# A DLRM tower on one core: ten chunk turns spread over the pass, and the second gram packed in quadrants between compares

## The reference

```python
e = jnp.stack([tbl_0[ids[:, 0]], ..., tbl_31[ids[:, 31]]], axis=1)   # (2048, 32, 128)
dot_products = jnp.einsum('bfd,bgd->bfg', e, e)
z = dot_products[:, iu, ju]                       # the 496 pairs above the diagonal
h = jnp.concatenate([z, dense_ctx], axis=1)       # 496 + 16 = 512
h = jnp.maximum(h @ W_top1 + b_top1, 0.0)
h = jnp.maximum(h @ W_top2 + b_top2, 0.0)
y = h @ W_top3
```

## Time and profile before

| | |
|---|---|
| median of 3 runs | 629.28 us (628.71 to 630.79) |
| the profiled execution | 625.68 us |
| its span, first to last instruction | 623.8 us |
| mean granted TensorE clock | 0.88 |
| PE, DVE, ACT, POOL busy | 447.8, 256.7, 126.5, 327.2 us |
| one pass of the loop (the fourth of six, 345.3 to 417.6 us) | 72.3 us |

### The profile page before, as it was taken

One profiled execution on the slowest core, in us unless ns is written; L12 is line 12 of the kernel. 1 busy time (PEld: TensorE's weight loads), 2 busy tenths in 40 slices (PEclk: granted clock), 3 DMA queues, 4 the chain that ended last, 5 costly groups with the idle time before them and its releaser, 6 DMA issues.

```text
span 623.8 us, 11340 instructions
## 1 busy us (share of the span) xinstructions
PE 447.8 (72%) x4692; PEld 406.2 (65%) x4692; DVE 256.7 (41%) x486; ACT 126.5 (20%) x220; POOL 327.2 (52%) x324
## 2 busy tenths in 40 slices
PE   0766311685779677886669867896877867798988
PEld 0766200675768577775669866685867757698967
DVE  2686000374407453373515544073533635158420
ACT  2452000012212122112211221121221122113313
POOL 6787777256643776346662566436763366620000
PEclk9998655797889987897998878898888978999999
DMA  7996312033321233012240223113421123311000
GB/s 164 245 232 172 100 50 55 14 56 73 76 56 35 67 71 80 26 46 59 73 82 17 59 68 76 50 38 63 76 77 28 42 63 74 77 26 27 1 4 1
DMA packets 31294, 42.10 MB, mean 67 GB/s; under 512 B 11077, under 2 KB 24141, under 8 KB 31273
## 3 DMA queue, kind: packets, MB, share of 16 engines
q1 hardware_dynamic: 18936, 20.64, 15.5%
q0 software_dynamic: 10240, 20.99, 13.3%
q10 hardware_dynamic: 2096, 0.17, 0.3%
HBM read 41.77 MB, written 0.01 MB: 67 GB/s over the span
## 4 chain that ended last, share of the span: by engine, by line
PE 50%; issue 15%; DVE 13%; another core or an unknown queue 12%; POOL 7%; DMA 2%; DVEq 0%; ACT 0%; POOLq 0%
PE sel_ps L289 19%; PE gram_ps L308 13%; PE work_ps L342 8%; POOL gathered L240 7%; DVE onehot L614 7%; DVE pairs L631 6%; PE work_ps L350 4%; PE work_ps L271 2%; DMA gathered<-table,tile_ids 2%; PE work_ps L420 1%; PE work_ps L333 1%; PE gram_ps L317 1%; PE work_ps L429 1%; PE work_ps L325 1%
## 5 line engine op out<-in xcount | busy, mean ns | idle before, releaser
L240 POOL DMA_INDIRECT gathered<-table,tile_ids x320 | 327.0, 1022 | 227.7 <-PE work_ps L271 110.1
L289 PE MATMUL sel_ps<-onehot,table_hi 125*128 125x256 f32 x768 | 213.6, 311 | 82.8 <-DVE onehot L614 36.8
L289 PEld LDWEIGHTS sel_ps<-onehot,table_hi 125*128 125x128 f32 x768 | 163.0, 212 | 90.5 <-issue 49.1
L614 DVE TENSOR_SCALAR onehot<-id_rows,row_no 128x512 fp32r<-128x512 int32 x384 | 160.2, 484 | 141.8 <-remote 80.3
L289 PE MATMUL sel_ps<-onehot,table_lo 125*128 125x256 f32 x768 | 206.9, 303 | 3.6 <-issue 3.6
L289 PEld LDWEIGHTS sel_ps<-onehot,table_lo 125*128 125x128 f32 x768 | 163.1, 212 | 6.6 <-issue 6.4
L631 DVE STREAM_TRANSPOSE pairs<-gram_ps 32x1024 f32<-32x1024 f32 x56 | 69.8, 1246 | 174.8 <-PE gram_ps L308 174.2
L308 PE MATMUL gram_ps<-rows_T 128*64 128x64 f32 x1792 | 80.5, 249 | 62.1 <-issue 62.1
L308 PEld LDWEIGHTS gram_ps<-rows_T 128*64 128x64 f32 x1792 | 72.3, 162 | 73.4 <-issue 73.0
L479 ACT ACTIVATE rows_T<-sel_ps 128x512 f32<-128x512 f32 x48 | 30.1, 627 | 221.5 <-remote 90.4
L470 ACT ACTIVATE rows_T<-work_ps 128x512 f32<-128x512 f32 x80 | 45.7, 594 | 136.7 <-PE work_ps L271 118.6
(11 more groups left out here) (26 smaller groups left out, 95.3 us busy)
## 6 DMA issues: line engine op xcount, KB each, us to landing
id_rows<-ids_selected SPq DMA_DIRECT2D x48, 256.0 KB
gathered<-table,tile_ids POOLq DMA_INDIRECT x320
pairs<-tables_selected SPq DMA_DIRECT2D x6, 448.0 KB
x<-tables_selected SPq DMA_DIRECT2D x6, 448.0 KB
w_sb<-w SPq DMA_DIRECT2D x1, 1024.0 KB
w_sb<-w SPq DMA_DIRECT2D x1, 512.0 KB
pairs<-tables_selected SPq DMA_DIRECT2D x6, 52.0 KB
x<-tables_selected SPq DMA_DIRECT2D x6, 52.0 KB
```

Of the source, the lines that this page charges most:

```text
L240: nc.gpsimd.indirect_dma_start(gathered[:, t, g, :], None, tables_gathered[g], bass.IndirectOffsetOnAxis(ap=slot_id, axis=0)).then_inc(chu ...
L289: last_op = nc.tensor.matmul(sel_ps[:, u % 2, e, :], part[0:SEL_P, 2 * u + e, k, :], onehot[0:SEL_P, h, kk, e, :], start=(e == 0 and k == ...
L614: last_op = nc.vector.tensor_scalar(onehot[:, h, kk, :, :].rearrange("p e s -> p (e s)"), id_rows[:, slot, :, :].rearrange("p e s -> p (e ...
```

## The change

The ten turns are put singly between the other work of PE. The new order of a pass is: turn 0; select 1; turn 1; pairs 0; select 2; turn 2; select 3; turn 3; select 4; turn 4; pairs 1; select 5; turn 5; first half of layer 1; turn 6; gram 0; turn 7; second half of layer 1; turn 8; select 0 of the next pass; turn 9; layer 2; gram 1; layer 3. The banks of `work_ps` are given out anew, and each turn from the third on waits for the move of the chunk before it. ScalarE's order follows.

On VectorE the pack falls into three functions. Gram 0 is still turned and merged at once, between compares 0 and 1 of the next pass. Gram 1 is turned in the next pass: two quadrants ahead of compare 2, one ahead of compare 3, one ahead of compare 4, and merged ahead of compare 5. The wait for `x0_done` is gone. In the last pass gram 0 is formed as in the loop (64 columns for each matmul) and no longer as singles. The diff:

```diff
--- before.py
+++ after.py
@@ -120,8 +120,8 @@
         gram_ps = psum("gram_ps", [P, 4 * 16 * N_FEAT])
         work_ps = psum("work_ps", [P, 2, CHUNK, P])
 
-        chunk_bank = [0, 1, 0, 0, 1, 0, 0, 1, 0, 1]
-        pairs_bank = [1, 1]
+        chunk_bank = [0, 1, 1, 0, 1, 1, 1, 1, 1, 1]
+        pairs_bank = [0, 0]
 
         def layer_ps(bank, n):
             return work_ps[:, bank, 2 * n:2 * n + 2, :].rearrange("p a s -> p (a s)")
@@ -248,25 +248,16 @@
                 first, n = CHUNKS[c]
                 pe.wait_ge(chunk_in[t][c], at(i, o, 16 * n, 16 * n))
 
-                if cc == 0 and not known_first(i, o):
-
-                    pass
-                elif cc == 1 and not known_first(i, o):
+                if cc == 1 and not known_first(i, o):
 
                     pe.wait_ge(sel_moved, at(i, o, UNITS, 1))
-                elif cc in (3, 6, 8):
-                    pe.wait_ge(chunk_moved, at(i, o, 2 * NC, {3: 3, 6: 6, 8: 7}[cc]))
-                elif cc == 2:
-                    pe.wait_ge(chunk_moved, at(i, o, 2 * NC, 1))
-                elif cc == 5:
-                    pe.wait_ge(chunk_moved, at(i, o, 2 * NC, 4))
-                elif known_first(i, o) and cc > 1:
-
-                    pe.wait_ge(chunk_moved, {4: 2, 7: 5, 9: 8}[cc])
-                elif cc in (4, 7):
-                    pe.wait_ge(x0_ready, at(i, o - 1, 2, {4: 1, 7: 2}[cc]))
-                elif cc == 9:
-                    pe.wait_ge(x1_ready, at(i, o - 1, 2, 1))
+                elif cc == 3 and known_first(i, o):
+                    pe.wait_ge(chunk_moved, 1)
+                elif cc == 3:
+                    pe.wait_ge(x0_ready, at(i, o - 1, 2, 1))
+                elif cc >= 2:
+
+                    pe.wait_ge(chunk_moved, at(i, o, 2 * NC, 3 if cc == 4 else cc))
                 for g in range(n):
                     last_op = nc.tensor.transpose(work_ps[:, chunk_bank[cc], g, :], gathered[:, t, first + g, :],
                                                   ident[:, :])
@@ -292,10 +283,10 @@
                                                            stop=(e == 1 and k == SEL_K - 1 and part is table_lo))
                     last_op.then_inc(onehot_used, 1)
 
-            def gram_waits(i, o, t, both=False):
+            def gram_waits(i, o, t):
                 pe.wait_ge(chunk_moved, at(i, o, 2 * NC, NC * (t + 1)))
                 pe.wait_ge(sel_moved, at(i, o, UNITS, UNITS))
-                if not (known_first(i, o) and t == 0) and not (both and t == 1):
+                if not (known_first(i, o) and t == 0):
 
                     pe.wait_ge(gram_read, at(i, o, 2, t))
 
@@ -339,7 +330,7 @@
                 for n in range(2):
                     for k in range(K1):
                         first = (2 * m + n) * P
-                        last_op = nc.tensor.matmul(layer_ps(1 - m, n), w1_sb[:, k, first:first + P],
+                        last_op = nc.tensor.matmul(layer_ps(0, n), w1_sb[:, k, first:first + P],
                                                    x0[:, k, :], start=(k == 0), stop=(k == K1 - 1))
                 last_op.then_inc(x1_done, 1)
 
@@ -351,36 +342,31 @@
                                                    x1[:, k, :], start=(k == 0), stop=(k == K2 - 1))
                 last_op.then_inc(x2_done, 1)
 
-            def selects(i, o):
+            def chunks_and_units(i, o):
 
                 turn(i, o, 0)
+                select(i, o, 1)
                 turn(i, o, 1)
-                select(i, o, 1)
-                turn(i, o, 2)
-                pe.wait_ge(chunk_moved, at(i, o, 2 * NC, 2))
+                pe.wait_ge(chunk_moved, at(i, o, 2 * NC, 1))
                 turn_pairs(i, o - 1, 0, pairs_bank[0])
                 select(i, o, 2)
+                turn(i, o, 2)
+                select(i, o, 3)
                 turn(i, o, 3)
+                select(i, o, 4)
                 turn(i, o, 4)
-                select(i, o, 3)
+                pe.wait_ge(chunk_moved, at(i, o, 2 * NC, 4))
+                turn_pairs(i, o - 1, 1, pairs_bank[1])
+                select(i, o, 5)
                 turn(i, o, 5)
-                pe.wait_ge(chunk_moved, at(i, o, 2 * NC, 5))
-                turn_pairs(i, o - 1, 1, pairs_bank[1])
-                select(i, o, 4)
+
+                pe.wait_ge(x0_ready, at(i, o - 1, 2, 2))
+                layer1(i, o - 1, 0)
                 turn(i, o, 6)
-                turn(i, o, 7)
-                select(i, o, 5)
-                turn(i, o, 8)
-
-            def layer1_first(i, o):
-
-                pe.wait_ge(x0_ready, at(i, o - 1, 2, 2))
-                pe.wait_ge(chunk_moved, at(i, o, 2 * NC, 8))
-                layer1(i, o - 1, 0)
 
             def layer1_second(i, o):
 
-                pe.wait_ge(chunk_moved, at(i, o, 2 * NC, 9))
+                pe.wait_ge(x1_ready, at(i, o - 1, 2, 1))
                 layer1(i, o - 1, 1)
 
             for u in range(UNITS):
@@ -388,7 +374,7 @@
                 select(0, 0, u)
                 if u == 1:
                     pe.wait_ge(ident_in, 16)
-                for cc in ((), (0, 1), (2,), (3, 4), (5,), (6, 7))[u]:
+                for cc in ((), (0,), (1, 2), (3, 4), (5,), (6, 7))[u]:
                     turn(0, 0, cc)
             turn(0, 0, 8)
             gram_waits(0, 0, 0)
@@ -399,18 +385,19 @@
             gram_part(1, 0, P // 4).then_inc(gram_done, 1)
             pe.wait_ge(weights_in, 80)
             with pe.Fori(0, n_pairs - 2) as i:
-                selects(i, 1)
-                layer1_first(i, 1)
-                layer1_second(i, 1)
+                chunks_and_units(i, 1)
                 gram_waits(i, 1, 0)
                 gram_part(0, 0, 32).then_inc(gram_done, 1)
+                turn(i, 1, 7)
+                layer1_second(i, 1)
+                turn(i, 1, 8)
+                select(i, 2, 0)
                 turn(i, 1, 9)
                 layer2(i, 0)
-                select(i, 2, 0)
-
-                layer3(i, 0)
                 gram_waits(i, 1, 1)
                 gram_part(1, 0, 32).then_inc(gram_done, 1)
+
+                layer3(i, 0)
 
 
             def layer1_tile(t):
@@ -439,14 +426,15 @@
                                                start=(k == 0), stop=(k == K3 - 1))
                 last_op.then_inc(y_done, 1)
 
-            selects(0, last)
-            layer1_first(0, last)
+            chunks_and_units(0, last)
+            gram_waits(0, last, 0)
+            gram_part(0, 0, 32).then_inc(gram_done, 1)
+            turn(0, last, 7)
             layer1_second(0, last)
-            gram_waits(0, last, 0, both=True)
-            gram_singles(0)
+            turn(0, last, 8)
             turn(0, last, 9)
             layer2(0, last - 1)
-            gram_waits(0, last, 1, both=True)
+            gram_waits(0, last, 1)
             gram_singles(1)
             layer3(0, last - 1)
 
@@ -491,7 +479,7 @@
                 act.wait_ge(x1_done, at(i, o, 2, m + 1))
 
                 for n in range(2 * m, 2 * m + 2):
-                    last_op = nc.scalar.activation(x1[:, n, :], layer_ps(1 - m, n % 2), ACT.Relu,
+                    last_op = nc.scalar.activation(x1[:, n, :], layer_ps(0, n % 2), ACT.Relu,
                                                    bias=b1_sb[:, n:n + 1])
                 last_op.then_inc(x1_ready, 1)
 
@@ -515,23 +503,23 @@
             def step(i, o):
 
                 move_chunk(i, o, 0)
+                move_unit(i, o, 1)
                 move_chunk(i, o, 1)
-                move_unit(i, o, 1)
-                move_chunk(i, o, 2)
                 move_x0(i, o - 1, 0, pairs_bank[0])
                 move_unit(i, o, 2)
+                move_chunk(i, o, 2)
+                move_unit(i, o, 3)
                 move_chunk(i, o, 3)
+                move_unit(i, o, 4)
                 move_chunk(i, o, 4)
-                move_unit(i, o, 3)
+                move_x0(i, o - 1, 1, pairs_bank[1])
+                move_unit(i, o, 5)
                 move_chunk(i, o, 5)
-                move_x0(i, o - 1, 1, pairs_bank[1])
-                move_unit(i, o, 4)
+                move_x1(i, o - 1, 0)
                 move_chunk(i, o, 6)
                 move_chunk(i, o, 7)
-                move_unit(i, o, 5)
+                move_x1(i, o - 1, 1)
                 move_chunk(i, o, 8)
-                move_x1(i, o - 1, 0)
-                move_x1(i, o - 1, 1)
                 move_chunk(i, o, 9)
                 move_x2(i, o - 1)
 
@@ -616,21 +604,23 @@
                                                           row_no[:, k:k + 1], None, ALU.is_equal)
                     last_op.then_inc(onehot_ready, 1)
 
-            def pack_pairs(i, o, t, singly=False):
+            def turn_gram(i, o, t, q):
+
+                if q == 0:
+
+                    dve.wait_ge(gram_done, at(i, o, 2, t + 1))
+                quadrant = slice(32 * q, 32 * q + 32)
+                last_op = nc.vector.transpose(pairs[quadrant, t, :, :],
```

(59 more changed lines are left out.)

## The result

The changed kernel takes 622.07 us (median of 5 runs, 620.44 to 624.17), against 629.28 us (627.57 to 630.79) for the kernel before on the same chip: ratio 0.987, 95% interval 0.984 to 0.990. That is 1.3% faster: 7.2 us, of the 21 forecast, and clear of the interval. The profiled execution took 620.44 us (span 618.5), against 625.68 (span 623.8).

The account below looks back on a forecast made before the run. No engine alone was the bound; 22.4 of PE's 23 us lost per pass arise while gathers move. Terms sum to 69.0 us against 72.3, saving 19.8 over six passes, plus 1.9 in the last: 608 us, range 583 to 643.

Parts of the forecast that it names:

- Five cycles of selects: Selects 1 to 5 with turns in the new pass: 6.2 us a cycle, between 5.2 and 7.0, so 31.0 us.
- First half of layer 1 and turn 6: The stretch of PE's pass between the select cycles and gram 0: 3.9 us.
- Gram 0: Gram beside gathers of chunks 5 and 6: 11.0 us, bounds 3.95 and 13.5, against 9.85 before.
- Turn 7 to layer 2: Stretch between the grams: 12.3 us of work plus 1.8 for one late signal before turn 9, 14.1 us.
- Gram 1: Gram losing its cover, with chunks 8 and 9 gathered beside it: 8.0 us, bounds 3.95 and 10.
- Layer 3: Last work of PE's pass, behind gram 1: 1.0 us.
- Part 1: VectorE's pack split among the compares: the wait before select 2 goes, gaining 1.9 us a pass, bounds 0 and 1.9.
- Part 3: First and last pass: first 0, bounds -3 and +3; last gains 1.9 us before select 2, bounds 0 and 3.
- What would show it: Signs: POOL's idle per pass from 19.8 to some 16.5 us, at each chunk; turns 5 to 7 us apart.
- rival B: Slower: interference moves from selects into grams, if a select cycle exceeds 6.7 us; pass 74.6 us, 641 us; chance 0.32.
- My own case: Spread turns and split pack shorten the loop's pass to 69.0 us: 608 us, own range 583 to 625; chance 0.52.
- Rival A: PE's lost 23 us a pass are scheduling; the pass falls to POOL's floor, some 54 us: 517 us; chance 0.08.

Follow-up runs that it names:

- the first gate: Changed kernel with POOL held from chunk 2 of the second pass until gram 0 of the first is done, against the kernel before: 603.91 us, 0.966.

## Why the prediction was right in direction and a third of the size

Putting the losses of the earlier trace rows down to the gathers was right, and the runs without gathers confirm it; that it is signals which are held is not shown apart from a crawling PE. The train's end is not always the end of it either: in the first pass POOL's last gather ends at 107.94, but gram 0 goes on one matmul at a time until its last 63 start together at 114.84. The step that failed is the price of the work that stands beside the gathers in the new order, above all of gram 0: put at 11.0 us, measured 12.9 on the mean of six passes. The sizes, by the prediction's terms and the pass above (73.6 us; the mean is 71.5):

- *Five cycles of selects, 31.0 us:* 29.7. Right in the sum (mean of six 29.1), though not as five cycles of 6.2: four run at PE's pace, and one waits 4.5 us for a late signal and then runs its select in 6.3 us instead of 4.1.
- *First half of layer 1 and turn 6, 3.9 us:* 5.5 (mean 5.3). The half layer is slowed and split by 0.3 us of crawl, 4.3 us in place of 3.5, and turn 6 waits 0.5 for ScalarE.
- *Gram 0, 11.0 us (bounds 3.95 to 13.5):* 13.3 (mean 12.9). No other term came out further above its price. I took a value inside where the nearest behaviour, eight gathers beside the gram, was the upper bound.
- *Turn 7 to layer 2, 14.1 us:* 14.2 (mean 14.0), with a late signal (1.2 us) counted in it, though ahead of gram 1 and not of turn 9.
- *Gram 1, 8.0 us (bounds 3.95 to 10):* 9.2, mean of six 8.9. That it loses its cover was right; the price is near what gram 0 paid in the earlier trace rows.
- *Layer 3, 1.0 us:* 1.7, at a granted clock of 0.50 (1.0 us in the earlier trace rows); so in three of the six passes, in the other three it takes 1.0. The forecast had no term for work that runs slowly beside or behind a crawl, and by the busy times given above (20 us more in the grams, beside 32 us of waits) that is a good part of the loss.

Gram 0, the half layer, gram 1 and layer 3 add 2.3 + 1.6 + 1.2 + 0.7 = 5.8 us to the 69.0, the selects take back 1.3. That pass is slower than any of the kernel before. On the mean of six the four terms are 1.9 + 1.3 + 0.9 + 0.4 = 4.5 us above their prices, the selects 1.9 and the stretch from turn 7 0.1 below; the pass is 2.5 us above my 69.0, and 6 x 2.5 = 15 us is the miss in the loop (a saving of 4.4 us where 19.8 was forecast).

*Part 1, 1.9 us a pass.* The wait before select 2 is gone, but the kernel with only this part gained 1.7 us in all (0.997). The lower bound that I had named holds: a held signal takes the wait's place. PE's waits in the selects of the six passes still sum to 57.5 us there, against 59.7. Without gathers the wait removed is real, 1.6 to 2.0 us.

*Part 3.* The first pass 0: +1.0, inside the bounds. The last pass -1.9: -1.9, in part by luck: PE's idle time in it falls by 3.1 us (the 1.6 before select 2 and 2.3 in the grams that are now formed otherwise, less what is new), and its busy time rises by 1.2.

*What would show it.* POOL's idle time did not fall to 16.5 us a pass. It is 73.6 - 40.2 - 12 = 21.4 in this pass, 17.6 in the one before it and 19.7 on the mean, as before. Nor does it lie at each chunk: the trains are of four or eight gathers (of twelve before) with 1.9 to 6.4 us between. The turns stand 4.3 to 5.3 us apart, but 11.2 where select 3 lies between, 13.9 over gram 0 and 16.2 over gram 1. The select cycles took 5.9 us on the mean (four of them 5.1 or less, that of select 3 11.2), so rival B's condition failed as a mean and held for one cycle in five, but its mechanism (the interference moves into the grams) is what ate the gain: 36 us of waits leave the selects and 32 appear in the grams. My own case and B were one mechanism at two strengths. Rival A is excluded on the first chip by passes of 71.5 us, and is what binds on the chip without the hold.

What stays open: whether plain transfers would hold PE if POOL issued them in trains as long as those of the gathers; why the indirect gathers hold PE on some chips (the kernel before at 624 to 629 us in four groups of runs) and not on another (472 us in two), and what in PE is held, since a crawling PE and late signals look alike from the profile. That the gain was 1.3% on one chip and 2.8% on another is not explained beyond one thing: on the second, select 3 starts in two pieces, after waits of 1.0 and 1.9 us in the pass shown (2.9 us in each of the six), instead of after one of 4.5 (3.8 to 4.5). No version run that computes everything beats the change by more than its interval; the first gate was not run beside it on one chip that has the hold.

## What to carry to other kernels

When an engine loses time beside another engine's instructions, rearranging moves the loss to whatever then stands beside them. Before forecasting a gain from an order, price each piece of work at what it costs beside the disturber, and take the worst measured price, slower work included, unless something reduces the disturber itself. A kernel run with the disturber removed separates the two at once: 3.0 us of good order a pass, of which 0.7 arrived. And a stall whose releaser is "issue", ended together with a train on another engine, should be tried on a second chip before a kernel is tuned around it.

## What the hardware showed that I had not expected

- The same kernel takes 624 to 629 us in four groups of runs and 471 to 474 us in two on another chip; the changed one 607 to 622, and 467.
- The hold was seen with the indirect form alone: 69 to 71 us a pass with indirect gathers and 68 to 70.5 with contiguous rows in that form on one chip; 48.0, on another with the kernel before at 625 us, with plain transfers of the same size from the same queue, which leave POOL idle for half of the time.
- An indirect gather of 128 rows occupies POOL for 1.02 us, with 0.30 us of issue ahead of it; a plain transfer from POOL takes 0.57 us.
- How far PE gets in a gram before it crawls: 28 to 36 matmuls in the six passes of the kernel before, 46 to 61 in eleven of the twelve grams of the changed kernel (21 in the other).
- Without gathers, a wait of 1.6 to 2.0 us ahead of select 2 is followed by a granted clock of 1.00 in three passes and of 0.69 in three others, after the same work (4.1 and 5.6 us for the select).
